# Reading the convolution's input from PSUM in a four-layer kernel

## What is computed

```python
zxbcdt = u @ W_in.T
z = zxbcdt[..., :D_INNER]
xBC = zxbcdt[..., D_INNER:D_INNER + CONV_DIM]
dt = zxbcdt[..., D_INNER + CONV_DIM:]
dt = jax.nn.softplus(dt + dt_bias)
xc = lax.conv_general_dilated(xBC.transpose(0, 2, 1), W_conv, (1,), [(D_CONV - 1, 0)],
                              dimension_numbers=('NCH', 'OIH', 'NCH'), feature_group_count=CONV_DIM)
xBC = jax.nn.silu((xc + b_conv[None, :, None]).transpose(0, 2, 1))
x = xBC[..., :D_INNER].reshape(b, L, NHEADS, HEADDIM)
...
Y, _final = ssd_minimal_discrete(x_scaled, A_dt, Bm, Cm, CHUNK)
y = Y + x * D[None, None, :, None]
g = y * jax.nn.silu(z)
y = g * lax.rsqrt(jnp.mean(g * g, axis=-1, keepdims=True) + EPS) * norm_w
return y @ W_out.T
```

## Time and profile before

| | us |
|---|---|
| median of 3 runs | 1397.97 (1394.99 to 1403.28) |
| the profiled execution | 1401.69 |
| its span, first to last instruction | 1399.5 |
| PE busy | 1288.1 (92%) |
| DVE busy | 959.6 (69%) |
| ACT busy | 613.2 (44%) |
| POOL busy | 547.5 (39%) |

### The profile page before, as it was taken

How to read it: one execution, slowest core, us unless ns; L and a number is a source line. 1 busy time by engine, 2 the same in 40 slices (tenths; PEclk the granted TensorE clock), 3 DMA queues, 4 the chain that set the end, 5 groups by cost and what they waited for, 6 DMA issues and landing times. The chain is left out here.

```text
span 1399.5 us, 20257 instructions
## 1 busy us (share of the span) xinstructions
PE 1288.1 (92%) x7032; PEld 1048.9 (75%) x7032; DVE 959.6 (69%) x1630; ACT 613.2 (44%) x1108; POOL 547.5 (39%) x521
## 2 busy tenths in 40 slices
PE   6699999999999999998998988989989799999994
PEld 6577888888888888887665655656656688888884
DVE  3487635444445453436688888788797799999997
ACT  3243323232323232335757657656663444444431
POOL 1254200000000000001476576575676457677765
PEclk9899999999999999999999999998999899999997
DMA  5122001010100000000010010010110100000000
GB/s 181 45 77 94 31 1 30 1 31 0 31 1 30 0 15 30 8 8 11 16 34 24 27 34 15 26 41 7 34 41 8 46 1 30 30 30 30 30 16 30
DMA packets 30392, 41.27 MB, mean 29 GB/s; under 512 B 2433, under 2 KB 22913, under 8 KB 30209
## 3 DMA queue, kind: packets, MB, share of 16 engines
q1 hardware_dynamic: 30336, 40.53, 8.8%
HBM read 27.94 MB, written 12.58 MB: 29 GB/s over the span
## 5 line engine op out<-in xcount | busy, mean ns | idle before, releaser
L1047 DVE TENSOR_TENSOR hb<-gl,bank 128x512 f32<-128x512 f32 x128 | 88.0, 687 | 199.0 <-PE bank L46 196.4
L657 ACT ACTIVATE hh<-hb 128x512 fp32r<-128x512 f32 x128 | 80.9, 632 | 182.5 <-DVE hb L1047 182.5
L696 ACT ACTIVATE gl<-bank 128x512 f32<-128x512 f32 x128 | 76.6, 598 | 179.5 <-PE bank L46 179.4
L1010 DVE TENSOR_TENSOR hl<-hb,hh 128x512 fp32r<-128x512 f32 x128 | 95.9, 749 | 84.5 <-ACT hh L657 84.5
L524 POOL TENSOR_TENSOR veb<-mvb,eps 128x4 f32<-128x4 f32 x8 | 1.8, 230 | 349.9 <-DVE mvb L1027 349.9
L1139 DVE SCALAR_TENSOR_TENSOR acc<-raw,cw,acc 128x512 f32<-128x512 f32 x108 | 110.6, 1024 | 19.1 <-ACT acc L761 16.5
L44 PE MATMUL bank<-xt_l,w_h 128*128 128x512 f32 x256 | 105.0, 410 | 16.1 <-DVE xt_l L1010 14.2
L640 POOL TENSOR_TENSOR dhl<-dab,dhh 128x512 fp32r<-128x512 f32 x64 | 100.4, 1591 | 30.6 <-ACT dhh L657 30.6
L44 PE MATMUL bank<-at_l,w_hi_a 128*128 128x512 f32 x256 | 103.3, 403 | 1.3 <-DVE at_l L1010 1.0
L45 PE MATMUL bank<-xt_h,w_l 128*128 128x512 f32 x256 | 103.6, 405 | 0.0
L46 PE MATMUL bank<-xt_h,w_h 128*128 128x512 f32 x256 | 103.5, 404 | 0.0
(11 more groups left out here) (217 smaller groups left out, 3866.1 us busy)
## 6 DMA issues: line engine op xcount, KB each, us to landing
xg<-x_scratch SPq DMA_DIRECT2D x16, 512.0 KB, 4.0
xall<-in_x SPq DMA_DIRECT2D x8, 512.0 KB, 7.8
...
```

The source lines that it names most:

```text
L657: return act.activation(dst, src, ACT.Copy)
L696: act.activation(gl[:, n % 2], ps_gate[n % 2][:], ACT.Gelu_apprx_tanh).then_inc(s_gelu, 1)
L1010: return dve.tensor_tensor(dst, src, hi.bitcast(F32), ALU.subtract)
L1047: dve.tensor_tensor(hb[:, n % 2], gl[:, n % 2], ps_up[n % 2][:], ALU.mult).then_inc(s_h, 1)
```

## The change

`raw` and its copy are gone. ACT keeps only the last three columns of the bank in `tail` (128x3) and forms the last tap's term as before; DVE's three taps read the bank in PSUM, shifted by 3, 2 and 1 columns, and so write 509, 510 and 511 columns. What the three first columns get from the group before, POOL works out for all five blocks in five small instructions (`halo_terms`, into `hfix`, 128x5x3), in chunk 0, and DVE adds it with one small instruction to each block (128x3) ahead of the taps. A bank is thus held until the taps are done. For this the projections get a third bank: `ps_x` moves into the bank of `ps_yoff`, its own becomes `lane_a`, and `ring` becomes a table of lanes. With it go new waits on PE: `ps_yoff` waits for ACT's copy of `ps_x`, the transposes to `ps_x` for `yo`, z tiles 0 and 1 and segment sum 1 for a convolution in their lane. The decay sums move behind the segment sums, and the convolution of block 4 moves on DVE from chunk 3 part 0 to chunk 2 part 1.

```diff
         bank = [ctx.enter_context(nc.psum_tensor(f"bank{i}", [P, 512], F32)) for i in range(8)]
         ps_gate, ps_up, ps_down, ps_t = bank[0:2], bank[2:4], bank[4:6], bank[6:8]
-        small, ps_x, ps_y, ps_yoff, ps_ds, ps_g = bank[2:8]
-        def ring(i):
-            return bank[i % 2]
+        small, ps_y, ps_yoff, ps_ds, ps_g = bank[2], bank[4], bank[5], bank[6], bank[7]
+        ps_x = ps_yoff
+        lane_a, lane_b, lane_c = bank[3], bank[1], bank[0]
+        T_LANE = (lane_b, lane_a)
+        DT_LANE = lane_c
+        XBC_LANE = (lane_b, lane_a, lane_c, lane_b, lane_a)
+        Z_LANE = (lane_c, lane_b, lane_b, lane_c)
+        SEG_LANE = (lane_c, lane_a, lane_b, lane_c)
+        ACS_LANE = lane_a
...
+            def halo_terms(n, b):
+                if not isinstance(n, int) or n > 1:
+                    pool.wait_ge(c_xin, XB * (n - 1))
+                weight = [cw[:, :, tap:tap + 1].broadcast_to([P, XB, TAPS - 1 - tap]) for tap in range(TAPS - 1)]
+                pool.tensor_tensor(hfix[:, b], tail[:, b], weight[0], ALU.mult).then_inc(c_fix, 1)
+                pool.tensor_tensor(hpart[:, 0, :, 0:2], tail[:, b, :, 1:3], weight[1], ALU.mult).then_inc(c_fix, 1)
+                pool.tensor_tensor(hpart[:, 1, :, 0:1], tail[:, b, :, 2:3], weight[2], ALU.mult).then_inc(c_fix, 1)
+                pool.wait_ge(c_fix, FIX * n + 2)
+                pool.tensor_tensor(hfix[:, b, :, 0:2], hfix[:, b, :, 0:2], hpart[:, 0, :, 0:2], ALU.add).then_inc(c_fix, 1)
+                pool.wait_ge(c_fix, FIX * n + 4)
+                pool.tensor_tensor(hfix[:, b, :, 0:1], hfix[:, b, :, 0:1], hpart[:, 1, :, 0:1], ALU.add).then_inc(c_fix, 1)
+            pool.memset(tail[:], 0.0).then_inc(c_init, 1)
+            pool.wait_ge(c_init, 1)
+            halo_terms(0, 0)
...
+                    if nxt and c == 0:
+                        halo_terms(nxt[0], nxt[1])
...
-                src = place if place is not None else ring(XBC0 + j)
+                src = place if place is not None else XBC_LANE[j]
                 act.wait_ge(c_xbc, XB * n + j + 1)
                 if place is None:
                     act.wait_ge(c_silu, XB * n + max(j - 1, 0))
-                copy(raw[:, j, TAPS - 1:], src[:])
+                act.wait_ge(c_fix, FIX * (n + 1))
+                copy(tail[:, b, j], src[:, TOK - TAPS + 1:])
                 act.activation(xc[:, b, j] if in_xc else acc[:, j % 2], src[:], ACT.Identity, bias=cb[:, j:j + 1],
                                scale=cw[:, j, TAPS - 1:TAPS]).then_inc(c_xin, 1)
...
             def x2_hi(n, b):
-                act.wait_ge(c_cv, (TAPS - 1) * XB * n)
-                act.wait_ge(c_halo, 2 * n)
-                copy(raw[:, :, 0:TAPS - 1], tail[:, b]).then_inc(c_halo, 1)
                 for k in range(KT):
                     act.wait_ge(c_t, KT * n + k + 1)
-                    copy(xt_h[:, k], ring(k)[:]).then_inc(c_xth, 1)
...
-            def keep_tail(n, b):
-                act.wait_ge(c_xin, XB * (n + 1))
-                act.wait_ge(c_halo, 2 * n + 1)
-                copy(tail[:, b], raw[:, :, TOK:]).then_inc(c_halo, 1)
...
-                    decays(n, b)
                 if slot == 3 and part == 0:
                     segment_exp(n, 1)
                     segment_exp(n, 2)
                     segment_exp(n, 3)
-                    keep_tail(n, b)
+                    decays(n, b)
                     conv_silu(n, b, 4)
...
-            act.wait_ge(c_init, 1)
-            keep_tail(0, 0)
             dt_exp_ln(0, 0, mid=False)
-            decays(0, 0)
             for t in range(NT):
                 segment_exp(0, t)
+            decays(0, 0)
...
-            def conv(n, b, j, in_xc=False):
+            def conv(n, b, j, in_xc=False, in_early=False):
                 sums = xc[:, b, j] if in_xc else acc[:, j % 2]
+                src = early(j) if in_early else XBC_LANE[j]
                 dve.wait_ge(c_xin, XB * n + j + 1)
-                dve.wait_ge(c_halo, 2 * n + 1)
+                dve.wait_ge(c_fix, FIX * (n + 1))
+                dve.tensor_tensor(sums[:, 0:TAPS - 1], sums[:, 0:TAPS - 1], hfix[:, b, j], ALU.add).then_inc(c_cv, 1)
                 for tap in range(TAPS - 1):
-                    steps = (TAPS - 1) * (XB * n + j) + tap
-                    if tap > 0:
-                        dve.wait_ge(c_cv, steps)
-                    dve.scalar_tensor_tensor(sums, raw[:, j, tap:tap + TOK], cw[:, j, tap:tap + 1], sums, ALU.mult, ALU.add).then_inc(c_cv, 1)
+                    late = TAPS - 1 - tap
+                    dve.wait_ge(c_cv, TAPS * (XB * n + j) + tap + 1)
+                    dve.scalar_tensor_tensor(sums[:, late:], src[:, 0:TOK - late], cw[:, j, tap:tap + 1], sums[:, late:],
+                                             ALU.mult, ALU.add).then_inc(c_cv, 1)
             def dt_chain(n, b, mid=True):
...
-                if slot > 0 and (slot < 3 or part == 0) and not (slot == 2 and part == 1):
-                    conv(n, b, {(1, 0): 1, (1, 1): 2, (2, 0): 3, (3, 0): 4}[slot, part])
+                if slot in (1, 2):
+                    conv(n, b, {(1, 0): 1, (1, 1): 2, (2, 0): 3, (2, 1): 4}[slot, part])
...
-                            pe.wait_ge(c_xin, j - 1)
+                            pe.wait_ge(c_cv, TAPS * (j - 1))
...
             def z_proj(n, t):
                 if t < 2:
-                    pe.wait_ge(c_xin, XB * n + 4 + t)
+                    pe.wait_ge(c_cv, TAPS * (XB * n + 3 + t))
                 else:
                     pe.wait_ge(c_e, NT * n + t + 1)
-                tok_proj(z_place(t)[:], t, slice(0, D_INNER)).then_inc(c_zp, 1)
+                tok_proj(Z_LANE[t][:], t, slice(0, D_INNER)).then_inc(c_zp, 1)
             def decay_sums(n):
-                pe.wait_ge(c_zs, NT * n + 1)
-                pe.wait_ge(c_dtc, DT_STEPS * (n + 1))
+                pe.wait_ge(c_e, NT * n + 2)
                 flat = adt[:].rearrange("p t h -> p (t h)")
-                pe.matmul(ring(ACS0)[:, 0:16], upto[:], flat, start=True, stop=True)
-                pe.matmul(ring(ACS0)[0:D_STATE, 16:32], ones[:], flat, start=True, stop=True).then_inc(c_acs, 1)
+                pe.matmul(ACS_LANE[:, 0:16], upto[:], flat, start=True, stop=True)
+                pe.matmul(ACS_LANE[0:D_STATE, 16:32], ones[:], flat, start=True, stop=True).then_inc(c_acs, 1)
             def segment_sums(n, t):
                 if t == 0:
+                    pe.wait_ge(c_zs, NT * n + 1)
+                    pe.wait_ge(c_dtc, DT_STEPS * (n + 1))
+                elif t == 1:
+                    pe.wait_ge(c_cv, TAPS * XB * (n + 1))
+                elif t == 2:
                     pe.wait_ge(c_zs, NT * n + 2)
-                elif t == 1:
-                    pe.wait_ge(c_ea, 2 * (n + 1))
                 else:
-                    pe.wait_ge(c_e, NT * n + t - 1)
+                    pe.wait_ge(c_e, NT * n + 1)
                 pe.wait_ge(c_au, NT * n + t + 1)
-                pe.matmul(ring(SEG0 + t)[:], below[:], au[:, t].rearrange("p h l -> p (h l)"),
+                pe.matmul(SEG_LANE[t][:], below[:], au[:, t].rearrange("p h l -> p (h l)"),
                           start=True, stop=True).then_inc(c_seg, 1)
             def in_proj_at(n, j):
-                if j == 1:
+                if j == 2:
                     pe.wait_ge(c_dtc, DT_STEPS * n + 1)
-                if j > 1:
-                    pe.wait_ge(c_xin, XB * n + j - 1)
-                in_proj(n, j, ring(XBC0 + j))
+                if j > 2:
+                    pe.wait_ge(c_cv, TAPS * (XB * n + j - 2))
+                in_proj(n, j, XBC_LANE[j])
...
-                    x2_transpose(n, b, i, ring)
+                    pe.wait_ge(c_ea, 2 * n)
+                    x2_transpose(n, b, i, lambda k: T_LANE[k])
                 if slot == 0 and part == 1:
...
                     z_proj(n, 1)
-                    decay_sums(n)
                     segment_sums(n, 0)
                 if slot == 3 and part == 0:
                     segment_sums(n, 1)
                     segment_sums(n, 2)
                     segment_sums(n, 3)
+                    decay_sums(n)
...
             def x_token_major(k, b, c):
                 pe.wait_ge(c_xtk, k + 1)
+                pe.wait_ge(c_yo, k + 1)
                 for h in range(HEADS):
...
                     pe.wait_ge(c_st, k + 1)
                     pe.wait_ge(c_yo, k + 1)
+                    pe.wait_ge(c_xtk, k + 1 + 1)
                     pe.matmul(ps_yoff[:], ct[:, b, cols], state[:, b].rearrange("p h d -> p (h d)"),
                               start=True, stop=True).then_inc(c_yoff, 1)
```

38 lines of the change are left out of this document (17 added, 21 removed).

## The result

The changed kernel takes 1392.76 us (median of 20 runs, 1387.52 to 1395.89), the kernel before 1399.84 beside it. The ratio is 0.9946, with an interval of 0.9935 to 0.9958: about 7.5 us, where 9.7 had been forecast. The profiled execution of the changed kernel has a span of 1385.8 us.

What follows compares the result with a forecast made beforehand. DVE's list, mostly convolution passes stretched by POOL, was taken to set the pace in each step's second half. 7 x 1.3 + 0.6 = 9.7 us, from the median of 1398.0 to 1388.3 (1383 to 1393 at 0.42; range 1377 to 1404).

Steps and rivals of the forecast that it cites:

- Taps: DVE's convolution passes reading PSUM: 0.74 to 0.75 us each, 2.33 for three, bounded by 2.2 and 3.5.
- Rival C: Taps from PSUM are dearer by 0.07 us a pass, 0.84 a step, 5.9 in all: 1394.2; chance 0.06.
- Rival E: Passes stay stretched by POOL; segment sum 1 goes to about 820.5; 31 us slower in all: 1429; chance 0.05.
- Block 2: Its convolution: addition waits 0.6, z tile 0 waits from about 802.4 until 804.4, PE reaches ps_ds 0.7 us ahead.
- Block 3: Its convolution on DVE: addition waits 0.2, ends at 808.6 instead of 810.95; DVE free at 812.5, 3.4 us ahead.
- Block 4: Its convolution, moved ahead of gm: addition held up 0.9, ends at 816.0; segment sum 1 starts 816.05 against 816.07.
- Rival A: Additions wait 1.3 us a step longer, using up the lead before segment sum 1; 9.1 us lost: 1397.4; chance 0.25.
- Behind it: After segment sum 1: exponential wait of 0.39 goes, decay sums take 0.45, ct's wait of 1.62 shrinks to 0.3.
- The step: One state-space step at full clock: 50.2 us instead of 51.5, 1.3 less.
- Rival B: More stretches at 1.2 GHz from PE's stalls; five of seven steps slow add 15.3 us: 1403.6; all seven 1413.8; chance 0.10.
- Ahead of the first step: ACT's table load for dt moves under its wait, ps_yoff waits for the first xtk; 0.6 us saved together.
- No price: halo_terms on POOL, ps_x and ps_yoff in one bank, and fewer ACT copies: no time charged for any.

Runs made afterwards that it cites:

- the filled kernel: The changed kernel with 12 extra matmuls of 128x512 on PE ahead of z tile 0 in chunk 2; ratio 0.9851 to the kernel before.

## Why the prediction was right, point by point

The forecast was 9.7 us, 1388; measured were 7.5. The terms of the sum can be read one by one.

**Taps**: right. A pass is 0.746 to 0.752, three are 2.32 (2.33 taken), none of 108 has a tail. Rival C (dearer passes) and with it the rule of the Trainium skill on PSUM sources (VectorE: DVE Perf Modes, the errata) did not come true here: a pass of 509 to 511 columns from PSUM has a median of 0.749, and the same passes from the SBUF copy 0.750. The term was read off loosely: `gg<-bank,xd` does not give the 0.96 GHz, since 256 columns more took 0.20 from the one row to the other, and 0.275 from `rows_out<-bank,rr` to the pass; that it came out at 0.75 leans on the undisturbed 0.752. Rival E, the slower side, is ruled out for this kernel. Its mechanism is what the one with the SBUF copy shows, at 12 us above the kernel before instead of 31.

**Block 2**: the mechanism right, the size too small, and this is the step that failed. z tile 0 on PE was to wait for about 2 us and waits 3.27. The prediction had DVE 0.4 ahead when block 2's convolution begins, 24.9 us after the step's start, and the addition held up for 0.6. It begins at 26.3, where it stood at 25.3 before. Two rows of the changed kernel's DVE and one of its POOL:

```profile
782.93 0.16 DVE L1137 TENSOR_TENSOR acc<-acc,hfix 128x3 f32<-128x3 f32 x1 [2.00 <-ACT acc L773]
...
788.42 0.68 DVE L1223 TENSOR_TENSOR mm_<-ee,gm 128x512 f32<-128x512 f32 x1
...
795.46 1.05 POOL L599 TENSOR_TENSOR xdc<-xsd,ee 128x512 f32<-128x512 f32 x1
```

and two of the DVE of before:

```profile
793.42 1.60 DVE L1220 TENSOR_TENSOR mm_<-ee,gm 128x512 f32<-128x512 f32 x1
...
801.33 0.41 DVE L1208 TENSOR_SCALAR rows_out<-rows_out,mv,rstd 128x256 f32<-128x256 f32 x1
```

First, the lead never came. Block 0's addition begins 12.65 us after the step's start; its first pass stood at 12.54 before. The 0.4 from ACT's missing copy was to bring it forward, and in this step did not; in two others it begins at 12.3. Second, the additions of blocks 0 and 1 cost 0.2 each with their gaps, and only the first had been counted. So DVE comes to the normalisation 0.4 later than before, at 25.3 instead of 24.9, now runs into POOL's `xdc`, and takes 1.05 instead of 0.41. Third, the addition behind it takes 0.99, most of it behind POOL's `au`. The stretched instruction of the dt chain (1.16) is no new loss: `mm_`, in the same chunk, took 1.60 before and takes 0.68 now. I had counted POOL's collisions with the additions of blocks 2 to 4 alone; but a collision that one instruction no longer has goes to another DVE instruction with all its operands in SBUF that stands there.

Together, block 2's last pass ends 29.6 us after the step's start, as before (29.7), where 28.0 had been forecast. And PE was to come to `ps_ds` 0.7 earlier than before by one stall taking the other's place. It comes 0.9 later at full clock (854.22 in the filled kernel's step from 823.16, 31.1 in, against 30.2) and 2.4 later where the clock falls. What the step gains, it gains behind that place: with block 4's passes gone from ahead of the state's update, DVE begins `ct` at 49.3 in the filled kernel instead of 50.8.

**Block 3**: the addition took 0.63, 0.4 of it waiting where 0.2 had been taken.

**Block 4**: the place right, the number wrong. 1.7 us of waiting at segment sum 1 were forecast, none was there, because PE comes later itself by what it lost at z tile 0. With that wait filled, PE does wait there, 0.90. So the lead was used up, but one place earlier than I said. Rival A, in which the additions are held up longer and use up the lead at segment sum 1, has a part of the loss, at the later place. That it had to be moved was not in the prediction at all: left behind `gm`, it makes PE wait 5.1.

**Behind it**: the 0.39 of waiting for an exponential did not go; it is 0.56, ahead of the decay sums. `ct` was to be waited for 0.3 and is for 0.6 to 0.9, since its copy went from 0.42 to 1.23. A wait of 0.66 for `btk` in chunk 1 is new.

**The step**: 50.2 forecast; 50.6 at full clock, in one step of the kernel with the wait filled (51.1 and 50.7 in others). From the 51.5 of before it is 0.9 instead of 1.3, and seven times 0.9 is 6.3. Stretches at 1.2 GHz cost 12.2 us in the steps before, by the prediction's reckoning; by the same one they cost 367.1 less 7 times 50.6, 12.9, now. 6.3 less 0.7 are the 5.6 measured. This is an estimate, with a step of another kernel in it.

**Rival B** (more stretches at 1.2 GHz) had 0.10 and was half right. The clock does fall at z tile 0, in seven steps of seven, for the reason given. What I had missed is that the scattered falls of before would go in exchange, so that the number stayed at nine and the time at the lower clock at about 41 us. The mark that I had set for it, three of seven steps with a clock below 0.92, was not reached: one has.

**Ahead of the first step**: 1.9 instead of 0.6. ACT's wait went as forecast; 1.1 more is that the segment sums ran less of their time at 1.2 GHz, 5.13 against 6.26, which had no term. It is no chance of one execution: the stretch is 16.1 to 16.3 in all seven kernels that have the changed one's list there, the one without additions included, and 18.0 in both of the old order; in the five with a sixth small instruction on POOL it is between 16.0 and 18.3. Why the clock is higher there is not shown.

**No price**: right. The five halo terms on POOL take 0.2 to 0.4 each, in chunk 0, and POOL's wait for `yo` is 0.5 behind them instead of 2.17. The shared bank was waited for once, 0.37 us in the first chunk.
